# Window attention with sinks: the value product of a pair of units split into two halves and moved behind the next scores in TensorE's order

## The reference

```python
mask = (j > i) | (i - j > WINDOW)                      # WINDOW = 128
logits = jnp.where(mask, -jnp.inf, einsum('bhqd,bhkd->bhqk', q, k) / sqrt(DH))
lse = jax.nn.logsumexp(logits, axis=-1, keepdims=True)
denom_log = jnp.logaddexp(lse, attn_sink.reshape(1, H, 1, 1))
attn = jnp.exp(logits - denom_log)
y = jnp.einsum('bhqk,bhkd->bhqd', attn, v)
```

## Time and profile before

| | us |
|---|---|
| median of three runs | 2917.28 (2906.43 to 2920.45) |
| the profiled execution, its own time | 2912.0 |
| its span, first to last instruction | 2910.2 |
| PE busy in the span | 2461.5 (85%) |
| DVE busy in the span | 2112.4 (73%) |
| ACT busy in the span | 1418.4 (49%) |

### The profile page before, as it was taken

The page is one execution under the profiler, slowest core; times in us unless marked ns, Lnnn a source line. Parts: engine busy times, 40 slices in busy tenths (PEclk is TensorE's granted clock), DMA queues, the critical chain, the costliest instruction groups (busy, mean ns, idle before and its releaser), DMA issues. The chain is left out here.

```text
span 2910.2 us, 41656 instructions
## 1 busy us (share of the span) xinstructions
PE 2461.5 (85%) x12267; PEld 1460.2 (50%) x12332; DVE 2112.4 (73%) x4148; ACT 1418.4 (49%) x3005; POOL 644.9 (22%) x621
## 2 busy tenths in 40 slices
PE   6994999759988888779995599999569888869998
PEld 4772344337755444457773422222136544437776
DVE  3984777449978878279995188888148788738998
ACT  2552455525512766246664036666510476615665
POOL 2324010013235000024444100000016300013443
PEclk7996899969979999889997779999879999979999
DMA  1213222112110000034432611211310000004443
GB/s 63 80 54 81 53 69 53 25 61 80 54 41 4 1 1 1 8 114 150 153 135 49 160 32 34 46 31 26 48 43 1 5 1 1 5 4 149 148 154 115
DMA packets 109526, 169.58 MB, mean 58 GB/s; under 512 B 58546, under 2 KB 80946, under 8 KB 98274
## 3 DMA queue, kind: packets, MB, share of 16 engines
q1 hardware_dynamic: 92468, 165.47, 19.0%
q10 hardware_dynamic: 16896, 2.10, 0.5%
HBM read 145.96 MB, written 12.78 MB: 55 GB/s over the span
## 5 line engine op out<-in xcount | busy, mean ns | idle before, releaser
L1482 DVE TENSOR_REDUCE b1x_maxima<-b1x_m_bank 128x1 f32<-128x512 f32 x512 | 317.8, 682 | 79.5 <-PE b1x_m_bank L1400 79.5
L1522 ACT ACTIVATE b1x_probs<-b1x_e_bank 128x1024 f32<-128x1024 f32 x256 | 248.3, 1021 | 118.0 <-PE b1x_e_bank L1418 110.9
L1482 DVE TENSOR_REDUCE a1x_maxima<-a1x_m_bank 128x1 f32<-128x512 f32 (+3 forms) x384 | 190.0, 550 | 69.6 <-PE a1x_m_bank L1403 45.4
L1400 PE MATMUL b1x_m_bank<-b1a_k_slot,b1a_q_slot 96*128 96x512 bf16 x512 | 190.9, 413 | 19.4 <-DMA b1x_v_slot<-b1a_v_aug 18.3
L1522 ACT ACTIVATE a1x_probs<-a1x_e_bank 128x1024 f32<-128x1024 f32 (+1 forms) x192 | 147.3, 809 | 99.5 <-PE a1x_e_bank L1421 76.2
L1418 PE MATMUL b1x_e_bank<-b1a_q_slot,b1a_k_slot 128*128 128x512 bf16 x475 | 146.2, 386 | 8.2 <-issue 4.1
L1434 PE MATMUL b1x_o_bank<-b1x_probs,b1x_v_slot 128*32 128x512 f32 x1024 | 137.8, 610 | 0.7 <-ACT b1x_probs L1522 0.7
L1400 PE MATMUL a1x_m_bank<-a1a_k_slot,a1a_q_slot 96*128 96x512 bf16 (+3 forms) x384 | 119.9, 350 | 19.3 <-DMA a1x_v_slot<-a1a_v_aug 17.7
L1400 PEld LDWEIGHTS b1x_m_bank<-b1a_k_slot,b1a_q_slot 96*128 96x128 bf16 x512 | 41.6, 98 | 177.5 <-DVE b1x_maxima L1482 131.6
L585 ACT ACTIVATE g2e_high<-g2e_hidden 128x512 fp32r<-128x512 f32 x128 | 81.0, 633 | 90.4 <-DVE g2e_hidden L618 90.2
L585 ACT ACTIVATE g1e_high<-g1e_hidden 128x512 fp32r<-128x512 f32 x128 | 81.0, 633 | 90.3 <-DVE g1e_hidden L618 90.2
(11 more groups left out here) (556 smaller groups left out, 6609.5 us busy)
## 6 DMA issues: line engine op xcount, KB each, us to landing
g1e_share<-scratch_combine SPq DMA_DIRECT2D x32, 1024.0 KB, 4.8
g2e_share<-scratch_combine SPq DMA_DIRECT2D x32, 1024.0 KB, 4.8
f1e_share<-scratch_combine SPq DMA_DIRECT2D x9, 1024.0 KB, 4.7
f2e_share<-scratch_combine SPq DMA_DIRECT2D x9, 1024.0 KB, 4.7
b1e_window<-scratch_bias_table SPq DMA_DIRECT2D x16, 320.0 KB, 4.8
a1a_k_slot<-scratch_k_parts SPq DMA_DIRECT2D x24, 192.0 KB
a1a_q_slot<-scratch_q_parts SPq DMA_DIRECT2D x72, 64.0 KB
b1a_k_slot<-scratch_k_parts SPq DMA_DIRECT2D x24, 192.0 KB
```

What stands on the lines that cost most here:

```text
L1400: mm = pe.matmul(bank[:, 0:width], q_slot[s][0:MAX_ROW, qt // 4, hh, chunk(qt % 4, 128)], k_slot[s][0:MAX_ROW, hh, k0:k0 + width], start=T ...
L1482: dve.tensor_reduce(maxima[:, k0 // NC, col:col + 1], bank[:, 0:width], AX, ALU.max).then_inc(m_taken, 1)
L1522: act.activation(probs[g % 2][:, 2 * pair:2 * pair + 2, 0:width], e_bank[pair][:, :, 0:width], ACT.Exp, scale=scale).then_inc(exp_done, 1)
```

## The change

TensorE's order is written anew. `out` now takes a key tile, and issues only the two matmuls of that key tile; its waits stand before the first half, its signal behind the second. TensorE's list becomes turn(u), score(u + 3), and then one half of a value product: the first half of pair (u - 2)/2 at an even u, the second at the odd u that follows. ScalarE's `copy_out` of a pair moves from an even to the next odd u.

```diff
-            def out(pair):
+            def out(pair, kt):
                 t, j = pair // 2, 2 * (pair % 2)
-                pe.wait_ge(copied0, 2 * pair + 2)
-                pe.wait_ge(copied1, 2 * pair + 2)
-                if pair >= 2:
-                    pe.wait_ge(out_copied, pair - 1)
-                for kt in range(2):
-                    for e in range(2):
-                        mm = pe.matmul(...)
-                mm.then_inc(out_done, 1)
-            score(0)
-            score(1)
-            for u in range(UNITS):
-                if u + 2 < UNITS:
-                    score(u + 2)
-                turn(u)
-                if u % 2 == 0 and u >= 2:
-                    out(u // 2 - 1)
-            out(UNITS // 2 - 1)
+                if kt == 0:
+                    pe.wait_ge(copied0, 2 * pair + 2)
+                    pe.wait_ge(copied1, 2 * pair + 2)
+                    if pair >= 2:
+                        pe.wait_ge(out_copied, pair - 1)
+                for e in range(2):
+                    mm = pe.matmul(...)
+                if kt == 1:
+                    mm.then_inc(out_done, 1)
+            for u in range(3):
+                score(u)
+            for u in range(UNITS + 2):
+                if u < UNITS:
+                    turn(u)
+                if u + 3 < UNITS:
+                    score(u + 3)
+                if u >= 2:
+                    out((u - 2) // 2, u % 2)
...
-                if u % 2 == 0 and u >= 2:
-                    copy_out(u // 2 - 1)
+                if u % 2 == 1 and u >= 3:
+                    copy_out((u - 3) // 2)
             copy_out(UNITS // 2 - 1)
```

More of the change, by code:

```diff
@@ L820, in turn @@
                 mm.then_inc(turned_done, 1)
-            def out(pair):
+            def out(pair, kt):
                 t, j = pair // 2, 2 * (pair % 2)
-                pe.wait_ge(copied0, 2 * pair + 2)
-                pe.wait_ge(copied1, 2 * pair + 2)
-                if pair >= 2:
-                    pe.wait_ge(out_copied, pair - 1)
-                for kt in range(2):
-                    for e in range(2):
[L831 to L834, removed]
-                mm.then_inc(out_done, 1)
-            score(0)
-            score(1)
-            for u in range(UNITS):
-                if u + 2 < UNITS:
-                    score(u + 2)
-                turn(u)
-                if u % 2 == 0 and u >= 2:
-                    out(u // 2 - 1)
-            out(UNITS // 2 - 1)
+                if kt == 0:
[4 more added lines that the diff above has]
+                for e in range(2):
+                    mm = pe.matmul(outs[pair % 2][64 * e:64 * e + 64, :],
+                                   v[:, t + kt, (j + e) * DH:(j + e + 1) * DH],
+                                   probs_T[(2 * pair + e) % 4][:, kt, :],
+                                   start=(kt == 0), stop=(kt == 1), skip_group_check=True)
+                if kt == 1:
[9 more added lines that the diff above has]
+                    out((u - 2) // 2, u % 2)
         @block.vector
```

## The result

The changed kernel takes 2867.9 us (median; 2865.54 to 2871.26) against 2914.39 for the kernel before (the three executions above and one more). The ratio is 0.9843, 95% interval [0.9815, 0.9871]: 1.6% faster. 2868 was forecast.

What follows compares the result with a forecast made beforehand. Order, not a full engine, sets the pace: the value product lies on the path. 59 x 3.57 = 210.6, plus 5.8 and 0.1, is 216.5 a stage; two stages save 49.0, 2917.3 becomes 2868; range 2853 to 2892.

Steps and rivals of the forecast that it cites:

- The stall and its place: Attention stages: the whole value product (1.87 us) stands before the scores, so VectorE waits once a pair, 44.5 us in all.
- "Three ahead": TensorE's list: score(u + 3) is only a way to write it; the sequence of turns and scores is unchanged.
- The unit of 3.57: TensorE per unit afterwards: turn to scores 0.93, scores to half 1.60, half 1.04; 3.57 us against 3.97.
- a cost of leaving of 0.13: End of a value product before a turn: 1.90 instead of 1.87 us, so changing matmul shape costs 0.13.
- one change of shape per pair that is new in kind: TensorE's list: only one change of matmul shape per pair differs in kind; taken at 0 extra.
- The sum: Turn 2 to turn 63: 216.5 us against 241.05, so 24.5 less a stage and 49.0 in two.
- The last two units: End of the stage, without scores: VectorE's 2.92 us binds, 5.8 us for both.
- The slack elsewhere: VectorE idles about 0.4 us a unit before its copy; ScalarE's exponentials have 0.86 us to spare.
- The exponentials: Rival: the stall on scores returns through ScalarE's exponentials and the gain does not come, 2917 us; chance 0.05.
- Dearer halves: Rival: entering or leaving a half of the value product costs 0.15 us more a unit, 2886 us; chance 0.12.
- The unpaired half: Rival: a half's two matmuls no longer run side by side; half 1.90, unit 4.43, 2970 us; chance 0.03.
- The clock: Rival: a nearly always busy TensorE is granted a lower clock; at 0.85 about 2943 us; chance 0.04.

Runs made afterwards that it cites:

- moved_whole: Changed kernel, but a pair's value product stands whole behind the even unit's scores, with `copy_out` back at the even unit; 2878.73 us, ratio 0.9858 to the kernel before.
- split_in_front: Changed kernel, but each half of the value product stands in front of the next scores; 2877.83 us, ratio 0.9854 to the kernel before.
- split_by_unit: Changed kernel, but a half is one unit's product over both key tiles, not one key tile for both units; 2963.11 us, ratio 1.0149 to the kernel before.
- no_mask: Changed kernel without the two mask matmuls of each unit, so the window is not applied; 2818.77 us, ratio 0.9666 to the kernel before.

## Why the prediction was right

- *The stall and its place.* That the whole product stands in front of the scores, and that VectorE waits for them once a pair, is shown from both sides: moving it away (moved_whole) and halving it (split_in_front) each won back most of the lost time, with pair times of 7.31 and 7.27 against 7.94 before and 7.06 with both.
- *"Three ahead" is nominal.* All versions keep the same sequence of turns and scores and the same two score tiles. The changed kernel, moved_whole, split_in_front and split_by_unit differ only in the place and size of the product's pieces (and in the `copy_out` that follows them), and that accounts for their stage times, but for the 1.6 us of clock in moved_whole.
- *The unit of 3.57.* It came out at 3.53. Turn to scores was 0.93 as said. Scores to the half took 1.58 (1032.38 to 1033.96) where 1.60 was taken from scores to a turn. The half took 1.01 to the next turn and not 1.04. That term was mis-sized by the row it was read from: in the earlier trace rows the product of 1175.21 is followed by the turn of 1177.11, which I read as a cost of leaving of 0.13. VectorE's timeline of the kernel before has the normalize that this turn needs:

```profile
1175.92 1.13 DVE L888 TENSOR_SCALAR h<-h,g1a_inv 128x256 f32<-128x256 f32 x4
```

  It ended at 1177.05 and held the turn, which starts 0.06 later, the distance of 0.05 that the prediction itself allows from normalize to turn. In moved_whole, where nothing holds the turn, the same whole product takes 1.87 to it (1035.66 to 1037.53). The 0.10 of the earlier trace rows, read before a mask, was the right one. The prediction speaks of one change of shape per pair that is new in kind. It is one in every unit, products of 64 rows to a half of 64 columns, so two a pair, and the sum has it in every unit. It costs no more than the others.
- *The sum.* The 59 steps took 208.2 us (3.528 each) where 210.6 was reckoned. That is 2.4 of the 2.5 us between the 27.0 measured and the 24.5 forecast; the last 0.1 is the one added for what follows the last turn, where nothing was lost. Two stages gave 54.0 and not 49.0. That the medians moved by only 46.5 is inside the scatter of the other phases. The hit to 0.1 us (2868 against 2867.9) is luck: the kernel before stood 2.9 us lower in the second median than in the one that the sum started from (2914.4 and 2917.3), and the medians fell by 2.5 less than the 49.0 forecast.
- *The last two units.* 2.93 and 2.92 apart, with TensorE waiting 0.82 us for normalize, as the chain turn, copy, normalize gives it.
- *The slack elsewhere.* VectorE was said to idle about 0.4 us a unit, and idles 0.35 (3.53 less 3.18), of which 0.26 is a wait that the profile names, a little under the 0.3 to 0.4 forecast for it. One more operation of 0.20 fitted in, the second did not fit whole. The exponentials did not come back as a wait: the sinks' one ends at 1035.09 and the mask that needs it starts at 1035.90, 0.81 us to spare where 0.86 was reckoned.
- *The rivals.* Dearer halves did not show. The unpaired half is real and was priced right (0.85 us a unit against 0.86), but the changed kernel's halves stay paired. The clock stayed at 1.00 from 936 to 1150 us.

## What to carry to other kernels

When an engine with slack still waits once per two steps, look for an item in another engine's list that comes only every second step and stands in front of what is awaited. Moving it behind and cutting it evenly are two remedies for the same stall: each alone takes most of it, and their gains do not add. Cut such an item along the dimension that keeps matmuls side by side on the array, and count the changes of matmul shape over the whole list, since two items of one shape next to each other save one.

Before a row is used as the price of a step, check that the instruction that follows it was not held by something else. And price an edit by the stage that it touches: here stages repeat to 0.3 us, but for one short drop of the clock, while the rest of the same code moves by 12 us from profile to profile.

## What the runs showed of the hardware that was not expected

- The added VectorE operation of 128x256 fp32 takes 0.20 us of the list, while its duration is given as 0.28 to 0.29 us. The four operations of normalize have the same shape and take 1.05 us together in the list (1033.18 to 1034.23 in the changed kernel), 0.26 each, with a duration of 0.35 each. Both take 0.08 to 0.09 us less of the list than their durations say, and the two kinds differ although their shapes do not, so neither a sum of durations nor one kind's price holds for the other.
- A TensorE shown as busy for 99.5% of a stretch (184.08 of 185.00 us in no_mask) was not the bound: it had about 0.09 us of slack in each unit of 3.18, which its busy time hardly shows.
